# A spiking attention block with a ternary feed-forward network on one core: the hand-laid orders of four engines, laid anew

## The reference

```python
def attn(x):                       # x normalised over channels first
    z  = layer_norm(x, ln1_s, ln1_b); zz = time_shift(z)
    k  = (z*tmk + zz*(1-tmk)) @ Wk;  v = (z*tmv + zz*(1-tmv)) @ Wv
    r  = sigmoid((z*tmr + zz*(1-tmr)) @ Wr)
    x  = x + lif((r * wkv(w_decay, u_first, k, v)) @ Wo)   # scan over time; spikes
    z  = layer_norm(x, ln2_s, ln2_b); zz = time_shift(z)
    kk = square(relu((z*f_tmk + zz*(1-f_tmk)) @ fWk))      # 128 -> 512
    return x + lif(sigmoid((z*f_tmr + zz*(1-f_tmr)) @ fWr) * (kk @ fWv))
def ffn(x):                        # hidden width 512, ternary weights, row scales
    h = silu(x @ w1.T * w1_s) * (x @ w2.T * w2_s)
    h = gelu(h @ h1.T * h1_s); h = gelu(h @ h2.T * h2_s)
    return h @ w3.T * w3_s
x = x + norm(attn(norm(x)))
x = x + norm(ffn(norm(x)))
```

## Time and profile before

| | |
|---|---|
| median of 3 runs | 709.31 us (706.81 to 709.71) |
| the profiled execution | 710.65 us |
| its span, first to last instruction | 708.5 us |
| mean granted TensorE clock | 0.949 |
| instructions | 10,945 |
| busy: PE, DVE, ACT, POOL | 613.5, 566.3, 482.4, 438.4 us |
| DMA | 16.82 MB, 7.6% of 16 engines on the main queue |

### The profile page before, as it was taken

How to read it: one execution, slowest core, us unless ns; L and a number is a source line. 1 busy time by engine, 2 the same in 40 slices (tenths; PEclk the granted TensorE clock), 3 DMA queues, 4 the chain that set the end, 5 groups by cost and what they waited for, 6 DMA issues and landing times. The chain is left out here.

```text
span 708.5 us, 10945 instructions
## 1 busy us (share of the span) xinstructions
PE 613.5 (87%) x2563; PEld 399.0 (56%) x2563; DVE 566.3 (80%) x1552; ACT 482.4 (68%) x718; POOL 438.4 (62%) x560
## 2 busy tenths in 40 slices
PE   1245589999999999999999999999999999999884
PEld 0012236666656566666666666656666666566753
DVE  3866779898989999998989898989889897936230
ACT  3636076877869595959687786959595968757261
POOL 4333454687877767676768677786767684635242
PEclk9758579999999999999999999999999999999897
DMA  7000000001010000001010101000000101000000
GB/s 271 23 8 16 1 15 17 16 15 31 16 31 17 30 16 12 18 15 30 15 30 15 30 15 30 15 30 16 17 15 1 30 1 31 16 0 16 1 15 16
DMA packets 26538, 16.82 MB, mean 24 GB/s; under 512 B 1152, under 2 KB 25728, under 8 KB 26240
## 3 DMA queue, kind: packets, MB, share of 16 engines
q1 hardware_dynamic: 26496, 16.34, 7.6%
HBM read 12.14 MB, written 4.19 MB: 23 GB/s over the span
## 5 line engine op out<-in xcount | busy, mean ns | idle before, releaser
L735 ACT ACTIVATE hid<-p_f,scale 128x512 f32<-128x512 f32 x128 | 86.6, 687 | 102.0 <-PE p_f L1634 101.7
L1634 PE MATMUL p_f<-b_lo,w_hi 128*128 128x512 f32 x256 | 114.0, 445 | 11.0 <-DVE b_lo L306 10.9
L1634 PE MATMUL p_f<-a_lo,w_hi 128*128 128x512 f32 x256 | 112.5, 440 | 2.8 <-DVE a_lo L306 1.0
L449 POOL TENSOR_TENSOR nd<-factors,pq 128x512 f32<-128x512 f32 x32 | 38.0, 1187 | 102.1 <-DVE pq L1065 102.1
L1634 PE MATMUL p_f<-a_hi,w_hi 128*128 128x512 f32 x256 | 101.0, 394 | 0.0
L1634 PE MATMUL p_f<-b_hi,w_hi 128*128 128x512 f32 x256 | 101.0, 394 | 0.0
L433 POOL TENSOR_TENSOR rstd<-var,minus_half 128x4 f32<-128x4 f32 x64 | 75.0, 1172 | 2.5
L1619 PE MATMUL p_m<-kk,mix 128*128 128x512 f32 x128 | 64.0, 602 | 9.5 <-issue 5.3
L1634 PEld LDWEIGHTS p_f<-b_lo,w_hi 128*128 128x128 f32 x256 | 48.1, 188 | 37.5 <-issue 25.7
L1792 PEld LDWEIGHTS p_turn<-w,hid 128*128 128x128 f32 x512 | 61.5, 200 | 12.3 <-DVE f_lo L1173 11.0
L1792 PE MATMUL p_turn<-w,hid 128*128 128x128 f32 x512 | 63.9, 285 | 2.3 <-DVE f_lo L1173 1.4
(11 more groups left out here) (135 smaller groups left out, 1506.8 us busy)
## 6 DMA issues: line engine op xcount, KB each, us to landing
xa<-in_x SPq DMA_DIRECT2D x16, 256.0 KB, 2.9
xb<-in_x SPq DMA_DIRECT2D x16, 256.0 KB, 2.9
out<-y_out SPq DMA_DIRECT2D x16, 256.0 KB, 3.0
kk<-in_ffn SPq DMA_DIRECT2D x1, 1024.0 KB, 7.1
hid<-in_ffn SPq DMA_DIRECT2D x1, 1024.0 KB, 9.6
mix<-in_mix SPq DMA_DIRECT2D x1, 512.0 KB, 6.5
gate<-in_ffn SPq DMA_DIRECT2D x1, 512.0 KB, 5.6
mix<-in_mix SPq DMA_DIRECT2D x1, 320.0 KB, 3.8
```

The costliest lines, as they stand in the source:

```text
L449: pool.tensor_tensor(nd[:, n], factors[:, 0], pq[:, n, :, 0:T], ALU.mult).then_inc(s_apq, 1)
L735: act.activation(hid[:, m], p_f[m % 2][:, :], ACT.Gelu, scale=scale[:, 1 + layer, m:m + 1]).then_inc(s_gelu[layer], 1)
L1634: last = pe.matmul(out_, w[:, b], x[:, k], start=(k == 0 and t == 0), stop=(k == n - 1 and t == len(terms) - 1))
```

## The change

The three lists of each of TensorE, VectorE, ScalarE and GpSimd are written in another order. The operations, the engine of each, the buffers and the banks are the same; the list of the DMA queue is not touched. Several steps change the turn in which they run: `ratio_end`, `neuron_input_2`, `voltage(1)`, `fire(1)`, `swiglu(1)`, `swiglu(2)`, `low(1, 0)`, `channel_v(3)`, `out_product`, `neurons(0)` and `variance(3)` move from the head of a turn to the tail of the one before; `log`, `inverse`, `to_value(2)` and `turn_1` move from a tail to the next head. `statistics` gets one wait. Lines behind it are numbered 3 to 5 higher.

```diff
@@ GpSimd, turn @@
-                if on[2]:
-                    neurons(0, g[2])
                 if on[4]:
                     low(2, g[4], 1)
-                if on[3]:
-                    variance(3, g[3])
-                    rstd(3, g[3])
...
                 if on[1]:
                     weighted_sum(g[1], 1)
                     weighted_sum(g[1], 0)
-                if on[4]:
-                    variance(5, g[4])
-                    rstd(5, g[4])
                 if on[0]:
                     norm_0(g[0])
-                if on[3]:
-                    low(1, g[3], 1)
                 if on[4]:
+                    variance(5, g[4])
+                    rstd(5, g[4])
                     norm_5(g[4])
+                if on[3]:
+                    low(1, g[3], 1)
...
+                if on[1]:
+                    neurons(0, g[1])
+                if on[2]:
+                    variance(3, g[2])
+                    rstd(3, g[2])
@@ ScalarE, turn @@
+                if on[3]:
+                    relu(g[3], 3)
+                if on[2]:
+                    log(g[2])
+                    inverse(g[2])
+                if on[3]:
+                    square(g[3], 3)
                 if on[4]:
                     silu_table()
@@ VectorE @@
             def statistics(n, g, bn, tiles):
+                wait(dve, s_mv[n], g.n)
                 for j in range(J):
                     last = dve.bn_stats(bn[:, j], tiles[:, j])
@@ TensorE, turn @@
                     if on[4]:
+                        to_value(g[4], 2)
                         to_gate(g[4], 3)
                         to_value(g[4], 3)
-                    if on[3]:
-                        channel_v(g[3], 3)
-                    if on[2]:
-                        out_product(g[2])
-                    if on[4]:
-                        hidden(1, g[4], 0)
-                        hidden(1, g[4], 1)
+                    if on[1]:
+                        turn_1(g[1])
                     if on[3]:
                         fired_sum(1, g[3])
                     if on[4]:
-                        hidden(1, g[4], 2)
+                        hidden(1, g[4], 0)
                     if on[3]:
                         spikes_turned(1, g[3])
+                    if on[4]:
+                        hidden(1, g[4], 1)
                     if on[2]:
                         fired_sum(0, g[2])
...
                     if on[1]:
                         k_product(g[1])
+                        r_product_1(g[1])
                     if on[4]:
                         hidden(2, g[4], 0)
                         hidden(2, g[4], 1)
-                        hidden(2, g[4], 2)
                     if on[2]:
                         turn_2(g[2])
-                    if on[1]:
-                        r_product_1(g[1])
...
+                    if on[2]:
+                        channel_k(g[2], 3)
                     if on[3]:
                         to_gate(g[3], 0)
                     if on[2]:
                         channel_v(g[2], 0)
-                        channel_k(g[2], 3)
+                        channel_v(g[2], 1)
+                        channel_v(g[2], 2)
+                        channel_v(g[2], 3)
                     if on[3]:
                         to_value(g[3], 0)
                         to_gate(g[3], 1)
...
+                    if on[1]:
+                        out_product(g[1])
```

477 lines of the change are left out of this document (234 added, 243 removed).

## The result

The changed kernel takes 713.59 us, the median of four runs (713.04 to 713.94); the kernel before, run beside it, 708.55 (706.81 to 709.71). The ratio is 1.008, 95% interval 1.0061 to 1.0099: slower by 0.8%, where 703.0 was forecast. The profiled execution has a span of 711.8 us; before it was 708.5. The changed kernel's four executions and the four of the kernel before do not overlap.

What follows compares the result with a forecast made beforehand. TensorE was taken to bound the steady turn, VectorE only 2 us behind. Steady turns -3.4, fill -1.7 and drain -2.5 sum to -7.6 us, from 710.65 to 703.0; forecast's own range 698 to 706.5, overall 690 to 716.

Steps and rivals of the forecast that it cites:

- (d): Added wait in `statistics`, five a turn: nothing can be late; taken as 0, bound 0.25 us a turn.
- My own sign of being wrong: First block of hidden layer 1 ends after T+17.5, or new holes stand between it and the next last product.
- T: Time in us since the last product (L1792) of a turn began on TensorE.
- the slower one: Rival: `norm_5` takes 4.55 us at its new GpSimd place, turn 39.2, kernel 718 us; chance 0.16.
- Steady turns: Turn goes from 38.26 to 38.0 us, -0.26, times 13: -3.4 us.
- fill: Start 3.7 us later, but products ahead of TensorE's branch free group 1's voltage scan: -1.7 us, bounds +3.7 and -3.
- drain: `norm_3` sooner, `turn_4` no longer waits (-1.0), clock may stay up (-1.5): -2.5 us, bounds 0 and -4.
- (a): Products moved as cover close TensorE's holes in the steady turn: -1.95 us a turn, bounds -1.95 and 0.
- (b): VectorE's later low halves end hidden layer 1's first block at T+16.6 to T+17.2; T+16.9 taken, +1.7 us a turn.
- (c): GpSimd's low half, now behind the output norm (`norm_5` 3.51 us), ends the same block at T+17.1, level with (b).
- (e): `log`, `inverse` and `square 3` pass over the turn's edge on ScalarE: costs nothing, covered by 0.2 us only.

Runs made afterwards that it cites:

- run 9: Kernel before with only the added wait in `statistics`, behind 48 semaphore increments at VectorE's start: 708.21 us, ratio 0.9994.
- run 8: Kernel before with only the added wait in `statistics`, all orders unchanged: 711.42 us, ratio 1.0049.
- run 5: Changed kernel with 48 semaphore increments at the start of VectorE's instructions, order unchanged: 707.07 us, ratio 0.9986.
- run 7: Kernel before with 24 semaphore increments at the start of VectorE's instructions, orders unchanged: 711.04 us, ratio 1.0042.
- run 13: run 5 with GpSimd's low part of block 1 of hidden layer 1 ahead of `norm_5` again, as before: 718.41 us, ratio 1.0153.
- run 3: Changed kernel with VectorE's turns 6 to 13 written out, so VectorE has no back edge: 707.01 us, ratio 0.9988.
- run 1: Changed kernel with VectorE's back edge moved ahead of `f0`, sequence of operations kept: 708.21 us, ratio 1.0004.
- run 2: Changed kernel with VectorE's back edge two operations later, behind the last gated product and a low part: 712.65 us, ratio 1.0072.
- Run 10: run 5 with, in the fill, VectorE's first norm of group 0 ahead of the statistics of group 1: 706.03 us, ratio 0.9973.
- run 11: run 5 with, in VectorE's last turns, block 1's spikes right behind their voltage: 707.05 us, ratio 0.9989.
- run 14: Run 10 with, in VectorE's steady turns, the next group's first norm ahead of `f0`: 705.90 us, ratio 0.9977.
- run 12: run 1 with block 1's spikes behind two low parts on VectorE, and TensorE's spike sums and transposes later to match: 719.39 us, ratio 1.0172.
- run 16: run 14 with 24 semaphore increments at VectorE's start instead of 48: 705.62 us, ratio 0.9962.

## Why the prediction was wrong, and where it was right

The side was wrong. The step that failed is (d), the wait added in `statistics`: "Nothing can be late", 0 to 0.25 us a turn. As a wait that holds (run 9). I priced what its instructions wait for and not where they push the loop, and no other step of mine has a term for that. The whole change moved VectorE's loop from 524 to 814 to 551 to 851. Of the 37 instructions by which the branch moved, 24 are that line's (run 8); the other 13 come from the order, so whether the changed kernel would fetch without the line stays open. Shown by runs 5, 7 and 8: the cost comes and goes with the position of the code at an unchanged order, 2.8 to 3.3 us for the kernel before and 6.5 for the changed one. By its wait an edge lengthens the turn by 1.4 us in both (39.7 against 38.27, 39.6 against 38.17). The changed kernel has 2.0 more at the middle edge, behind whose waits of 0.97 and 1.23 us the granted clock is 0.50. At the other two edges it waits 0.97 and 1.15, and 0.97 and 1.05, and the clock stays at 1.00; why it fell at one alone is not told. Where the other 1.2 us or more of the difference lie is not told. My own sign of being wrong came true at that edge: the first block of layer 1 ends at 345.79, T+18.8, past T+17.5. No rival of mine had the edge in it; the slower one, `norm_5`'s place, was another mechanism, and run 13 speaks against it.

The edges are not all of the miss. Without them (runs 3 and 5) the kernel takes 707.0 us, just outside the forecast's 698 to 706.5: by the medians the new orders are worth 1.2 us where I summed 7.6. Steady turns, fill and drain each gave less than I had put down, as told below.

Why the boundary lies where it does is inferred from counts. Loops that fetched: 541 to 832, 538 to 838, 548 to 838, 551 to 851, 554 to 855, 657 to 957. Loops that did not: 497 to 797, 524 to 814, 575 to 875, 586 to 886, 599 to 899. All fit boundaries 128 instructions apart (one between 558 and 575, one between 814 and 832, one between 942 and 957), and a loop that touches three such pieces stays, one that touches four is fetched anew at each edge. The straight code of run 3 agrees: by the traces' count about 807 instructions more than the changed kernel's, 6.3 pieces, and 31 packets where a loop that stays needs 25. The Trainium skill ("Runtime: NRT & Kernel Launch", "Instruction fetch mechanics") says that an engine holds two blocks of 16 KiB, 256 instructions each, and that a taken branch to a target outside them stalls for a fetch. That a stall comes from the branch's target, our runs bear out, and 32 KiB is four pieces of 128. The grain of 256 they do not. The loop from 541 to 832 touches three blocks of 256 only if a boundary lies between 541 and 576, the one from 657 to 957 only if one lies between 657 and 701; boundaries 256 apart can't do both, and both loops fetched. Why four pieces held do not keep a loop that touches four stays open.

The other steps, against the turns of the changed kernel without the edges:

(a) *Cover.* Right for the holes named. The steady turn no longer waits for b_lo, `mixed` or the transposes (0.67, 0.23 and 0.35 us in the earlier trace rows).

(b) *VectorE's way to hidden layer 1.* Right in time: in run 3 the last product starts at 287.24 and TensorE leaves the block at 303.98, T+16.7, where I took 16.9. I wrote that the sum of block 1's fired neurons "costs nothing more", and that holds: TensorE waits 0.97 us for it, but the fourth low half comes later still (its weight load waits for it until 303.40). What I had not seen is the sum of block 0's, one block on, for which TensorE waits 0.36. With that the turn closes: -1.95 + 1.5 + 0.36 is -0.1, and it is 38.15 to 38.17, -0.1 instead of -0.26.

(c) *POOL's way.* Fell. The norm takes 1.76 us at its new place, not 3.51, and TensorE does not wait for POOL's low part:

```profile
338.13 1.76 POOL L441 TENSOR_SCALAR f_out<-f_out,neg_mean,rstd 128x128 f32<-128x128 f32 x4 [0.20 <-POOL rstd L433]
339.86 1.70 POOL L306 TENSOR_TENSOR a_lo<-hid,a_hi 128x512 fp32r<-128x512 f32 x1
```

I had made this place a danger, and run 13 shows that the changed kernel loses 0.83 us a turn without it. By the rule of the Trainium skill that I set beside it ("SBUF — State Buffer", "SBUF: two separate sides") the estimate was 2.4 us, nearer to the 1.76 than my row's 3.51.

(e) *`log` and `inverse` over the edge.* Right: no wait for them appears in the steady turns.

*Fill:* -1.7 forecast, -0.24 seen in the two profiles, and even that is no gain to count on: the first last product comes at 134.4 to 134.9 us in the changed kernel and runs 1 to 3, at 131.8 to 134.9 in the kernel before and its variants. `norm_1` began at 13.94, the channel product and the output product came ahead of the branch (66.85 and 68.43; I had 65 and 66), and TensorE waited 4.19 us for the branch. But the voltage scan that I put at 72.7 came at 74.95. It was not freed from the branch: ahead of it VectorE copies the sum of fired neurons, and TensorE makes that sum behind the branch.

```profile
74.87 0.15 DVE L1114 COPY fired_all<-p_m 1x1 f32<-1x1 f32 x1 [3.66 <-PE p_m L1538]
```

Run 10 shows 1.0 us of the miss to be the norm's wait for the second tile, which I took for paid by what stood behind it. Why the fill of the kernel before varies by 3 us at an unchanged order is not told; the granted clock from 40 to 70 us was 0.73 in the profile with 134.9 and 0.78 in one with 131.9.

*Drain:* -2.5 forecast, -0.3 seen. The last product of turn 18 kept its clock and took 3.84 us instead of 6.78, -2.9 where I took -1.5, and `turn_4` no longer waits. What I missed is ahead of it: TensorE waits for VectorE's spikes and runs at half its clock just after, so the turn is 34.52 us instead of 32.45.

```profile
647.98 0.50 PE L1637 MATMUL p_m<-f_lo,w_hi 128*128 128x512 f32 x1 [0.47 <-DVE hid L1189]
...
649.94 0.16 PE L1538 MATMUL p_m<-fired,ones 128*128 128x1 bf16 x1 [1.22 <-DVE spikes L1107]
650.38 0.63 PE L1637 MATMUL p_f<-a_lo,w_hi 128*128 128x512 f32 x1 [0.28 <-issue]
650.81 0.63 PE L1637 MATMUL p_f<-a_hi,w_hi 128*128 128x512 f32 x1
```

The clock's loss was not removed: part of it moved from one turn to the one before (a granted clock of 0.54 from 650.3 to 654).

## What to carry to other kernels

Before pricing a change in a kernel with a hardware loop, count the instructions from the loop's head to its branch and where they lie, waits included, and read the instruction queues in the page's part 3: more packets with no more code is a loop that is fetched at each pass. Then compare turns with and without a back edge, since a mean over turns hides it. If a loop only just fits, write it out, or shift it, before judging an order by its time: here the same order measured 713.6 and 707.1 us. And a hole that goes from the engine that sets the pace is only gained once the next wait behind it has been looked for: three of my edits moved a wait; two won nothing that the medians show (runs 11 and 14), and one lost 11 us (run 12).

## What the runs showed of the hardware that I had not expected

A kernel became 6.5 us faster by 48 instructions that do nothing, and slower than at first by 106. VectorE's first operation began at 3.9 us without such increments and with 24 (run 16), at 5.2 with 48 and at 11.0 with 106, so beyond what the wait for its operand hides one costs about 0.1 us (5.8 us for 58). Taking a branch whose target had to be fetched took 2.8 to 3.1 us everywhere, 0.3 where it had not; the idle time behind it, 1.3 to 2.6 us, differed by the work issued ahead. Half a voltage scan took 0.65 or 1.46 us and `norm_5`, four instructions on POOL, 1.76 or 3.67 (run 13), by when they ran.
